# First expert's share of the value weights multiplied on GpSimd instead of ScalarE in the last section

## The reference

```python
pooled = hidden_states.mean(axis=1)
logits = jax.nn.relu(pooled @ Wg1 + bg1) @ Wg2 + bg2
vals, idx = jax.lax.top_k(logits, TOP_K)            # 2 of 4
sm = jax.nn.softmax(vals, axis=-1)
...
Wc = jnp.einsum('be,ecd->bcd', weights, W)          # per sequence b
bc = weights @ b
return jnp.einsum('btc,bcd->btd', hidden_states, Wc) + bc[:, None, :]
...
scores = jnp.einsum('bthd,bshd->bhts', q, k) / np.sqrt(D)
attn = jax.nn.softmax(scores, axis=-1)              # 16 heads of 16
out = jnp.einsum('bhts,bshd->bthd', attn, v)
return out.reshape(B, T, C) @ Wo + bo
```

## Time and profile before

| what | value |
|---|---|
| median of 3 runs | 1147.53 us (1144.92 to 1149.98) |
| the profiled execution's own time | 1141.54 us |
| its span, first to last instruction | 1139.7 us |
| busy share over the span: PE, DVE, ACT, POOL | 88%, 77%, 64%, 25% |
| last section, about 960 us to the end | some 180 us |

### The profile page before, as it was taken

The page is one execution under the profiler, slowest core; times in us unless marked ns, Lnnn a source line. Parts: engine busy times, 40 slices in busy tenths (PEclk is TensorE's granted clock), DMA queues, the critical chain, the costliest instruction groups (busy, mean ns, idle before and its releaser), DMA issues. The chain is left out here.

```text
span 1139.7 us, 27783 instructions
## 1 busy us (share of the span) xinstructions
PE 1000.3 (88%) x9262; PEld 815.5 (72%) x9262; DVE 872.6 (77%) x2482; ACT 724.1 (64%) x2778; POOL 286.7 (25%) x527
## 2 busy tenths in 40 slices
PE   6999967669999967878999979999997997889997
PEld 4888853247777843557777758999996986667775
DVE  5888989877888856975777755566655798689996
ACT  4887876768888866975777763112112544589995
POOL 4454530012222234422222210000000131333331
PEclk9999999679999997998999989999999998799999
DMA  9510000000000000005221000000000010000000
GB/s 282 133 30 1 3 1 1 0 15 16 15 12 11 11 2 1 0 6 130 85 82 52 10 2 1 0 0 0 0 1 19 24 29 6 5 12 14 14 14 20
DMA packets 43285, 30.17 MB, mean 26 GB/s; under 512 B 17208, under 2 KB 42432, under 8 KB 43200
## 3 DMA queue, kind: packets, MB, share of 16 engines
q1 hardware_dynamic: 43200, 29.10, 9.0%
HBM read 22.80 MB, written 2.10 MB: 22 GB/s over the span
## 5 line engine op out<-in xcount | busy, mean ns | idle before, releaser
L900 ACT ACTIVATE L1a_pr<-L1a_scores,L1a_nm 128x128 f32<-128x128 f32 x256 | 92.8, 415 | 4.5 <-DVE L1a_nm L989 3.8
L900 ACT ACTIVATE L2a_pr<-L2a_scores,L2a_nm 128x128 f32<-128x128 f32 x256 | 90.6, 390 | 6.0 <-DVE L2a_nm L989 6.0
L900 ACT ACTIVATE L0a_pr<-L0a_scores,L0a_nm 128x128 f32<-128x128 f32 x256 | 90.7, 395 | 4.4 <-DVE L0a_nm L989 4.4
L900 ACT ACTIVATION_READ_ACCUMULATOR L1a_pr<-L1a_scores,L1a_nm 128x1 f32 x256 | 65.1, 254 | 0.0
L989 DVE TENSOR_REDUCE L2a_nm<-L2a_scores 128x4 f32<-128x512 f32 x64 | 42.2, 683 | 24.9 <-PE L2a_scores L718 24.9
L2195 PE MATMUL L2f_inner<-L2f_taT,L2f_loraBT 128*128 128x128 f32 x512 | 59.7, 275 | 0.9 <-DVE L2f_hs L2347 0.9
L900 ACT ACTIVATION_READ_ACCUMULATOR L0a_pr<-L0a_scores,L0a_nm 128x1 f32 x256 | 60.1, 235 | 0.0
L2267 ACT COPY L2f_xTb<-L2f_xT 128x256 f32<-128x256 f32 x16 | 6.3, 411 | 84.5 <-PE L2f_inner L2184 84.5
L2184 PEld LDWEIGHTS L2f_inner<-L2f_xTb,L2f_wiT 128*128 128x128 f32 x512 | 58.3, 192 | 1.5 <-ACT L2f_loraBT L2151 1.2
L2184 PE MATMUL L2f_inner<-L2f_xTb,L2f_wiT 128*128 128x128 f32 x512 | 58.6, 275 | 0.9 <-ACT L2f_loraBT L2151 0.9
L2195 PEld LDWEIGHTS L2f_inner<-L2f_taT,L2f_loraBT 128*128 128x128 f32 x512 | 58.4, 192 | 1.1 <-issue 1.1
(11 more groups left out here) (621 smaller groups left out, 3147.2 us busy)
## 6 DMA issues: line engine op xcount, KB each, us to landing
L_ffn_w_w<-in_L_ffn_w SPq DMA_DIRECT2D x2, 1024.0 KB, 6.8
L1a_ctxT<-ctxT_all SPq DMA_DIRECT2D x16, 128.0 KB, 2.0
L2a_ctxT<-ctxT_all SPq DMA_DIRECT2D x16, 128.0 KB, 2.0
L3a_mem<-in_ctx SPq DMA_DIRECT2D x16, 128.0 KB, 2.1
out<-x_all SPq DMA_DIRECT2D x16, 128.0 KB, 1.7
L0a_ctx_nat<-in_ctx SPq DMA_DIRECT2D x1, 1280.0 KB, 12.4
x_all<-in_x SPq DMA_DIRECT2D x1, 1024.0 KB, 9.4
L_ffn_wi<-in_L_ffn_wi SPq DMA_DIRECT2D x1, 1024.0 KB
```

The source lines that it names most:

```text
L900: ex = act.activation(pr[q.s][:, j, h, :], S[j][:, h * P:h * P + P], ACT.Exp, bias=nm[q.s][:, j, h:h + 1], scale=-1.0, accum_out=ls[q.s][: ...
```

## The change

The share of lot 1 leaves ScalarE's step and is done by GpSimd, behind the bias addition. The new function multiplies with a TENSOR_TENSOR of the expert's columns and the gate, broadcast along the 768 columns, where ScalarE used an ACTIVATE with the gate as its scale. It raises the same semaphore, so VectorE's STT of lot 1 now waits for GpSimd. It waits for v of sequence b before it overwrites the tile. The shares of sequence 0, which ScalarE makes in the section before, stay there.

```diff
@@ gpsimd, step
                     if new:
                         add_bias(new)
+                    if mixed_here(new):
+                        before = new.earlier(2)
+                        mixing.share_by_pool(pool, new, before and (s_v[before.s], before.v))
@@ scalar, step
                     if pruned:
                         mine(prev, 3)
-                    if mixed_here(new):
-                        share(new, 1)
                     piece(cur, exp, 2)
@@ class Mixing
+    def share_by_pool(self, pool, q, before):
+        g, lot = self.g, self.lots[1]
+        first = pool.value_load(g.chosen[0:1, q.b, 0:1], min_val=0, max_val=3)
+        if before:
+            pool.wait_ge(*before)
+        width = lot.stop - lot.start
+        pool.tensor_tensor(self.mix[q.s][:, lot], g.experts[:, first, lot],
+                           g.gates[:, q.b, 0, :].to_broadcast([P, width]), ALU.mult
+                           ).then_inc(self.s_share[1][q.s], 1)
```

## The result

| | median | lowest to highest | runs |
|---|---|---|---|
| before | 1147.87 us | 1144.92 to 1149.98 | 6 |
| changed | 1155.36 us | 1152.65 to 1156.65 | 6 |

The ratio is 1.0069 (95%: 1.0058 to 1.0079): slower by 7.5 us between the medians, 7.9 by the ratio. The profiled execution of the changed kernel took 1156.65 us, its span is 1155.0.

A forecast was written before the change was run, and what follows sets the result against it. The loop was taken as v, share of lot 0, copy_x, k projection, kT, VectorE's list, v. 4.2 + 0.4 + 3.1 = 7.7 us on 1147.53 gave 1155.2 us, range 1150 to 1163.

The forecast's parts named there:

- The multiplication: GpSimd's new 768-column TENSOR_TENSOR behind the bias addition: claimed to take 1.46 us, with ends at 0.91 and 1.84.
- The steady stall: VectorE's STT of lot 1 waits 0.31 us for GpSimd in ten steps: 3.1 us, bounds 0 to 6.9.
- The relief of ScalarE: ScalarE loses 1.16 us a step, worth nothing; its wait for v grows from 0.61 to 1.77.
- The first steps: The late share of sequence 1 delays v and turn_x: 4.2 us, plus 0.4 for TensorE's lower clock.
- upper bound of 1.4: Clock term of the first steps: TensorE's 3.5 us stretch wholly at 1.2 GHz costs 1.4 more; 0.4 was taken.
- Steps 0 to 2: Counted nothing: step 0 hides its multiplication, step 1's 0.30 is taken up before v, step 2 ends in time.
- Had the multiplication taken 1.84: Rival of a later end, at the bias form's pace: steady stall 0.69, total 1159.7 us; later-end chance 0.31.
- had it been under 1.15: Rival of a short multiplication: no steady stall, only the first steps pay, about 1151.5 us; chance 0.15.
- ScalarE was not the bound before: Rival that ScalarE was the bound: each step wins up to 1.16 us, total 1134.8 us; chance 0.03.

The follow-up runs named there:

- the two kernels that remove it: The changed kernel with all shares first in GpSimd's step (1148.38 us, ratio 1.0015), and with the share behind kbd, ahead of the bias addition (1153.37 us, 1.0057).
- the one that keeps it alone: The changed kernel with the share of sequence 1 left on ScalarE, the other 14 on GpSimd: 1149.76 us, ratio 1.0023.
- the kernel with the shares at the head: The changed kernel with all 15 shares first in GpSimd's step, ahead of rlb and kbd: 1148.38 us, ratio 1.0015.
- The kernels of 32.25 and 33.37: All shares first in GpSimd's step, one prT copy moved to ScalarE: 1143.00 us; the same with the share of sequence 4 back on ScalarE: 1144.21 us.

## Why the prediction was right, step by step

**The multiplication** (1.46 by the line through `kbd`): 1.464. The two-input price of "GPSIMD Engine Reference" of the Trainium skill, § Performance versus the Vector engine, from which 1.85 was estimated, is not what this form took.

**The steady stall** (0.31, ten times, 3.1 us): 0.31 in each loop step, 97.99 against 95.02, so 3.0. That it is the stall and nothing else is shown by the two kernels that remove it, at 95.04 each, and by the one that keeps it alone, at 97.98.

**The relief of ScalarE** (nothing): shown by the kernel with the shares at the head. Only the size of the wait for v was off, 1.15 and not 1.77, because 0.77 us of idle came to lie ahead of the prT copy.

**The first steps** (4.2 + 0.4 = 4.6): kT of sequence 0 to kT of sequence 1 takes 15.29 us against 10.72, so 4.57. The sum came out right because the errors of its two terms cancelled, which is luck. `turn_x` stood 10.72 behind kT of sequence 0, before 7.11, so 3.6 later and not 4.2; the stretch from it to kT of sequence 1 grew from 3.61 to 4.57, so 0.96 and not 0.4. The first error has a reason in the rows: before, the STT of lot 1 held GpSimd in the middle of the late gates' factors; in the changed kernel that STT waits, the factors run through, and the bias addition comes 6.91 behind kT of sequence 0, not 7.65. The held row, and the same instruction in the changed kernel:

```profile
969.40 0.97 POOL L257 TENSOR_TENSOR kept_rstd<-late_gates_rs_t,kept_rstd 128x8 f32<-128x8 f32 x1
```

```profile
978.27 0.20 POOL L257 TENSOR_TENSOR kept_rstd<-late_gates_rs_t,kept_rstd 128x8 f32<-128x8 f32 x1
```

The second is the clock: the stretch ran at 0.50 from 982 to 990 us, and the k projection's 0.92 us more make up nearly all of it. The prediction had this case as its upper bound of 1.4.

**Steps 0 to 2** (nothing): in step 0 VectorE has no wait for GpSimd, as forecast. In step 1 the STT waits 0.31 us (forecast: 0.30 late), and VectorE's wait for TensorE ahead of v takes it up, as forecast: kT of sequence 2 to v takes 6.68 us in both kernels. In step 2 the STT waits 0.29 us, where the prediction had the multiplication end in time. What these steps cost can't be read finer than their clock allows: kT of sequence 1 to kT of sequence 4 takes 37.03 or 34.95 us in the two executions of before, and 35.88 or 35.79 in the changed ones. By the execution that the prediction read, the change gave back 1.15 us there; by the other it cost 0.9.

This is the one weak place of the sum. The kernel that differs from the changed one only in the share of sequence 1 shows what that share costs: its first four steps take 45.08 us, not 51.17, so 6.1 and not the predicted 4.6 (5.3 by the two ratios). Of this, 4.9 us lie ahead of kT of sequence 1, 1.4 in the stretch behind it, and the rest gives back 0.2. That stretch with its granted clock at the end of each row, ahead of the DMA columns, first in the changed kernel, then in the other one:

```profile
990.08:1002.52 12.44, 9.14 (x67) 7.95 (x71) 8.73 (x17) 6.21 (x28) 5.08 (x5) 0.86 0.00 0
```

```profile
984.39:995.44 11.05, 7.39 (x67) 6.17 (x70) 8.76 (x18) 6.86 (x32) 5.08 (x5) 1.00 0.00 0
```

The prediction let the cost of the clock end at kT of sequence 1, and in the execution that it read the stretch behind it was long already. So the mechanism was right in the main and the term of the first steps too small; that 7.7 came within 0.2 of the measured 7.5 to 7.9 is in part luck.

**The rivals.** Had the multiplication taken 1.84, the stall would have been 0.69; had it been under 1.15, none. Both are excluded by the 1.464. ScalarE was not the bound before; it becomes one as soon as a VectorE copy is given to it without the relief, as the kernel with the copy alone shows.

## What to carry to other kernels

Ask which loop closes a step, not which engine is fullest: 1.16 us a step taken off an engine as busy as the limiting one gained nothing until 0.6 us was also taken off the list that it waited for. A piece that is moved to an idle engine takes that engine's place in time, and in a pipeline's first steps that place can be far later than in the steady ones: here one of 15 shares cost 5 to 6 us, the ten in the loop 3. Before moving work to GpSimd, look at what VectorE does in the same microsecond, both ways.

## What was not expected of the hardware

- GpSimd held VectorE too: an 8x4 VectorE instruction of 0.15 us lasted 1.39 beside a multiplication of 1.47, and was back at 0.15 without it.
- The STT of lot 1 held GpSimd only while it ran: GpSimd's 8-column row took 0.97 us beside it, and 0.20 in the changed kernel, where the STT was still waiting.
- One and the same stretch of one kernel took 13.49 us at a granted clock of 0.75 and 11.04 at 1.00. A sum made against a single profiled execution carries that much.
- The drain took 31.0 to 31.1 us in every kernel with ScalarE's one prT copy, and longer in every kernel with more of them there. With one more it took 32.10 at a granted clock of 0.97 (steps of 9.75), 32.25 at 0.91 and 33.37 at 0.86 (steps of 8.91), with two more 34.58 at 0.92. The kernels of 32.25 and 33.37 ran the same work there, and TensorE was busy for 23.93 and 24.93 us in them, so their difference goes with the clock; how much of the rest is clock and how much the copy was not separated.
